# First unit's score products and maxima spread over the last two projection slots, with bands and steps loaded in another order

## The reference

```python
q, k, v = (shape(norm(x) @ W.T) for W in (Wq, Wk, Wv))        # (8, 16, 512, 16)
scores = einsum('bhqd,bhkd->bhqk', q, k) * 16**-0.5 + position_bias(rel_emb)
attn = softmax(scores, axis=-1)
x = x + einsum('bhqk,bhkd->bhqd', attn, v).transpose(...) @ Wo.T
x = x + ffn(norm(x))                                          # two of seven experts and a shared one
```

## Time and profile before

| | |
|---|---|
| median of three runs | 825.53 us (823.11 to 828.63) |
| profiled execution | 820.95 us, of which its span is 819.1 |
| mean granted TensorE clock | 0.958 |
| busy over the span | PE 94%, DVE 76%, PEld 67%, ACT 58%, POOL 32% |
| end of the projection block | 102.46 us from the start of the span |
| first exponent product | 123.69 us |

### The profile page before, as it was taken

How to read it: one execution, slowest core, us unless ns; L and a number is a source line. 1 busy time by engine, 2 the same in 40 slices (tenths; PEclk the granted TensorE clock), 3 DMA queues, 4 the chain that set the end, 5 groups by cost and what they waited for, 6 DMA issues and landing times. The chain is left out here.

```text
span 819.1 us, 18303 instructions
## 1 busy us (share of the span) xinstructions
PE 773.4 (94%) x6261; PEld 551.9 (67%) x6261; DVE 619.1 (76%) x1928; ACT 474.8 (58%) x716; POOL 260.6 (32%) x407
## 2 busy tenths in 40 slices
PE   4899989999999999999999999998997999999997
PEld 2677737566566566566565665777765589999974
DVE  4666487889889889888888884477865567777966
ACT  2344404766766766666666667466454267777730
POOL 1222111121121111111111111237777526666650
PEclk9999956999999999999999999988897999999999
DMA  4899883553364343453345284466632545556769
GB/s 117 229 351 360 304 259 109 135 145 100 101 170 137 116 123 106 151 169 101 99 121 152 81 267 136 166 187 206 212 101 85 175 133 165 161 158 208 222 202 355
DMA packets 74763, 140.77 MB, mean 172 GB/s; under 512 B 14651, under 2 KB 34771, under 8 KB 74497
## 3 DMA queue, kind: packets, MB, share of 16 engines
q1 hardware_dynamic: 62996, 116.12, 46.1%
q0 software_dynamic: 9792, 19.54, 7.4%
q10 hardware_dynamic: 1884, 3.97, 1.4%
HBM read 85.71 MB, written 56.78 MB: 174 GB/s over the span
## 5 line engine op out<-in xcount | busy, mean ns | idle before, releaser
L810 DVE CUSTOM_DVE_ANT_0 sums<-pS,near 128x512 bf16<-128x512 f32 x512 | 329.4, 688 | 48.4 <-PE pS L887 40.0
L847 ACT ACTIVATE prob<-pE 128x1024 f32<-128x1024 f32 x256 | 248.6, 1022 | 152.9 <-PE pE L912 152.8
L912 PEld LDWEIGHTS pE<-bandT,place 64*128 64x128 f32 x2048 | 167.4, 190 | 12.6
L912 PE MATMUL pE<-bandT,place 64*128 64x244 f32 (+2 forms) x2048 | 164.4, 272 | 0.0
L887 PE MATMUL pS<-k_st,q_st 48*128 48x512 f32 x512 | 139.0, 478 | 6.1 <-DVE nmax L810 2.5
L887 PEld LDWEIGHTS pS<-k_st,q_st 48*128 48x128 f32 x512 | 62.8, 193 | 115.6 <-DVE nmax L810 87.8
L926 PE MATMUL pC<-prob,v_aug 128*32 128x512 f32 x1024 | 135.7, 604 | 0.0
L904 PE MATMUL pE<-q_st,k_st 62*128 62x512 f32 x512 | 115.7, 407 | 1.4 <-issue 1.4
L1199 POOL DMA_INDIRECT expert_rows<-rb,xr x76 | 83.7, 1101 | 57.1 <-DVE rb L1414 45.5
L1184 POOL DMA_INDIRECT routed_rows<-xr,slot_i x64 | 66.2, 1034 | 32.2 <-issue 31.3
L1733 PE MATMUL pD<-w2p,hT 128*128 x456 | 63.5, 289 | 0.4 <-DVE hT L1407 0.4
(11 more groups left out here) (202 smaller groups left out, 1066.7 us busy)
## 6 DMA issues: line engine op xcount, KB each, us to landing
xr<-routed_rows SPq DMA_DIRECT2D x38, 258.0 KB, 2.9
q_st<-q_parts SPq DMA_DIRECT2D x64, 128.0 KB, 2.7
k_st<-k_parts SPq DMA_DIRECT2D x64, 128.0 KB, 2.9
ctx<-ctx_sb SPq DMA_DIRECT2D x32, 256.0 KB, 2.7
q_parts<-qk SPq DMA_DIRECT2D x14, 512.0 KB, 7.8
k_parts<-qk SPq DMA_DIRECT2D x14, 512.0 KB, 7.4
near<-bias_by_distance SPq DMA_DIRECT2D x16, 448.0 KB, 5.0
xr<-expert_rows SPq DMA_DIRECT2D x14, 512.0 KB, 4.3
```

The source lines that it names most:

```text
L810: dve.tensor_tensor_reduce(sums[:, r % 4], pS[:, unit % PS], near[:, hg % 2, j, lead:lead + S], -1.0, BIG, ALU.add, ALU.min, nmax[:, j, t: ...
L847: act.activation(prob[:, par, 2 * step:2 * step + 2], pE[:, 2 * (step % 2):2 * (step % 2) + 2], ACT.Exp).then_inc(exp_done, 1)
L912: ins = pe.matmul(pE[:, bank + side, a:z], place[rows, half], bandT[rows, (quad // 2) % 2, pair, part, lead:lead + z - a], start=False, st ...
```

## The change

Unit 0's scores and maxima move to the slots of batches 6 and 7: after each of their 8 groups m, TensorE issues one step of two products into the two banks `pB`, and VectorE takes its two maxima behind the low part of m. A product waits for the maximum two products earlier. `attend` begins with `turn(0)` on VectorE and with unit 1's scores on TensorE. `sums`, `nmax` and the two semaphores are now allocated ahead of both blocks.

SyncE's order is changed with it. The four tables `near` are loaded behind slots 1 to 4 (before, 2 to 5); step 0 behind slot 4, ahead of slot 5's load of x; steps 1 and 2 and the four bands behind slot 6, all within the projection block. In `attend` SyncE waits until unit 0's maxima have landed in the query tile, then loads step 3.

```diff
                 for b in range(B - 1):
                     slot(b, b % 2, b // 2, b < B - 2)
                     if b < 2:
                         load_rows(b)
-                    elif b < 2 + HPG:
-                        if b == 2:
-                            wait_apart(sp, passed, bias_stored, 16 * (4 + FARS))
-                        loads["near"](sp, 0, b - 2)
-                for m in range(4):
-                    wait_apart(sp, passed, qk_out[m], 16 * (B - 2))
-                wait_apart(sp, passed, v_out, 16 * (B - 2))
-                loads["step"](sp, 0, 0, True)
+                    if b == 1:
+                        wait_apart(sp, passed, bias_stored, 16 * (4 + FARS))
+                    if 1 <= b < 1 + HPG:
+                        loads["near"](sp, 0, b - 1)
+                    if b == HPG:
+                        stored(2)
+                        loads["step"](sp, 0, 0, True)
+                loads["step"](sp, 0, 1, True)
+                for j in range(HPG):
+                    loads["band"](sp, 0, j)
+                stored(B - 2)
+                loads["step"](sp, 0, 2, True)
...
                         dve.scalar_tensor_tensor(out=qk[:, m, 1], in0=pQ[:, m % 2, ORDER[m // 2]], scalar=SCALE if m < 2 else 1.0,
                                                  in1=qk[:, m, 0], op0=ALU.mult, op1=ALU.subtract).then_inc(qk_lo, 1)
+                        if first_step is not None:
+                            maxima(first_step + m)
...
+                def maxima(step):
+                    pair, t = divmod(step, TT)
+                    for side in range(2):
+                        unit, j = 2 * step + side, 2 * pair + side
+                        if t == 0:
+                            dve.wait_ge(g["near_ld"][j], 16)
+                        dve.wait_ge(g["s_mm"], unit + 1)
+                        if unit >= 4:
+                            dve.wait_ge(g["max_done"], unit - 3)
+                        lead = P * t
+                        dve.tensor_tensor_reduce(g["sums"][:, unit % 4], pB[:, unit % 2], g["near"][:, 0, j, lead:lead + S], -1.0, BIG,
+                                                 ALU.add, ALU.min, g["nmax"][:, j, t:t + 1]).then_inc(g["max_done"], 1)
...
+                def scores(step):
+                    pair, t = divmod(step, TT)
+                    if step == 0:
+                        pe.wait_ge(g["qk_ld"][0], 16 * 8)
+                        pe.wait_ge(bias_done, 2)
+                    for side in range(2):
+                        unit = 2 * step + side
+                        rows = slice(HALF * side, HALF * side + KQ)
+                        if unit >= 2:
+                            pe.wait_ge(g["max_done"], unit - 1)
+                        pe.matmul(pB[:, unit % 2], g["q_st"][rows, 0, pair, P * t:P * t + P], k_st[rows, 0, pair],
+                                  start=True, stop=True).then_inc(g["s_mm"], 1)
...
@@ attend, sync @@
-                loads["step"](sp, 0, 1, True)
-                for j in range(HPG):
-                    loads["band"](sp, 0, j)
-                for r in range(2, RING):
-                    loads["step"](sp, 0, r, True)
+                sp.wait_ge(max_ld, 32)
+                loads["step"](sp, 0, 3, True)
                 await_stores(sp)
@@ attend, vector @@
-                for ahead in range(STEPS * NI):
+                turn(0)
+                for ahead in range(STEPS, STEPS * NI):
@@ attend, tensor @@
-                for step in range(STEPS + LEAD):
-                    scores(step // STEPS, step // STEPS, 1, step % STEPS)
+                for step in range(LEAD):
+                    scores(1, 1, 1, step)
```

More of the change, by code:

```diff
@@ L189, in layer_kernel @@
             rows_set = sem("rows_set")
+            sums = sb("sums", [P, 4, S], BF16)
+            nmax = sb("nmax", [P, HPG, TT], F32)
+            s_mm, max_done = sem("s_mm"), sem("max_done")
             qk_out = [sem(f"qk_out{m}") for m in range(4)]
@@ L340, in load_rows, with stored @@
                                  ).then_inc(g["rows_set"], 16)
+                def stored(count):
+                    for m in range(4):
+                        wait_apart(sp, passed, qk_out[m], 16 * count)
+                    wait_apart(sp, passed, v_out, 16 * count)
                 for b in range(B - 1):
@@ L419, in normalised_lo, with slot @@
                         dve.tensor_tensor(xT[:, par, 1, c], pT[:, c], xT[:, par, 0, c], ALU.subtract).then_inc(loT, 1)
-                def slot(b, par, i, one, two):
+                def slot(b, par, i, one, two, first_step=None):
                     for m in range(4):
@@ L443, in _ @@
                         slot(2 * i + par, par, i, True, True)
-                slot(B - 2, 0, 3, True, False)
-                slot(B - 1, 1, 3, False, False)
+                slot(B - 2, 0, 3, True, False, 0)
+                slot(B - 1, 1, 3, False, False, TT)
             @block.scalar
@@ L499, in turn, with slot @@
                         ins.then_inc(xT_mm, 1)
-                def slot(b, par, one, first=False):
+                def scores(step):
[10 more added lines that the diff above has]
+                                  start=True, stop=True).then_inc(g["s_mm"], 1)
+                def slot(b, par, one, first=False, first_step=None):
                     pe.wait_ge(loT, 2 * b + 2)
@@ L510, in slot @@
                         ins.then_inc(qk_mm, 1)
+                        if first_step is not None:
+                            scores(first_step + m)
                     if one:
@@ L540, in _ @@
                         slot(2 * i + par, par, True)
-                slot(B - 2, 0, True)
-                slot(B - 1, 1, False)
+                slot(B - 2, 0, True, first_step=0)
+                slot(B - 1, 1, False, first_step=TT)
 def store_qk(engine, g, b, m):
@@ L655, in attend @@
         v_aug = sb("v_aug", [P, 2, TT, HPG, 32], F32)
-        sums = sb("sums", [P, 4, S], BF16)
-        nmax = sb("nmax", [P, HPG, TT], F32)
+        sums, nmax, s_mm, max_done = g["sums"], g["nmax"], g["s_mm"], g["max_done"]
         nparts = sb("nparts", [P, KM, HPG, TT], F32R)
@@ L663, in attend @@
         pC = ps("pC", [P, S], F32)
-        s_mm, max_done, split_done, max_turned, max_out, max_ld = (sem(n) for n in (
-            "s_mm", "max_done", "split_done", "max_turned", "max_out", "max_loaded"))
+        split_done, max_turned, max_out, max_ld = (sem(n) for n in (
+            "split_done", "max_turned", "max_out", "max_loaded"))
         e_mm, exp_done, pv_done, ones_set, v_ready, evac = (sem(n) for n in (
```

## The result

The changed kernel took 833.75 us (median of 13 runs, 824.86 to 841.46) against 822.12 us (818.91 to 830.03) for the kernel before in the same comparison: a ratio of 1.0115, 95% interval 1.0083 to 1.0146. Measured again beside the experiments (after_again), it was 830.66 against 825.04 us, 1.0055 (1.0027 to 1.0084). The ratios are taken over each kernel's fast executions alone, so they are not quotients of these medians. The change makes the kernel slower by some 0.5 to 1.2%. The forecast was 0.24% slower; its range, 820 to 835 us, is -0.7 to +1.15% of 825.53, so the second ratio lies well inside and the first at its very end.

The account below looks back on a forecast made before the run. VectorE's maxima, one pacing each product, were taken to bound the 21.2 us seam between projection and attention. +12.8 for a later block start, -11.5 in the seam, +0.5 near table: +1.8, taken as +2, 827.5 us; range 820 to 835.

Parts of the forecast that it names:

- The deciding step: SyncE's queue: step 0 ahead of x and the query store starts batch 6's first subtraction 2.6 us later, near 87.6.
- the 3.3 us for step 0's 1.0 MB in the transfer engines: Queues before batch 6: 2.6 us at a 512 KB store's pace, taken as 3.3 for smaller pieces, delaying x.
- the 0.5 us for the near table: Queues: one 448 KB table load moves one batch earlier; 0.5 us, between 0 and 1.2.
- The rounds on VectorE: Batch 6's slot: two maxima behind each low-part subtraction, three rounds of 1.95 us plus normalisation; 3.7 us more.
- Rival 2: Batches 6 and 7: the clock falls inside the projection and stays down; some +12 us, 837.5 us; chance 0.10.
- a clock below 1.00 before 105 us: New profile, TensorE's granted clock: listed among the signs that the forecast is wrong.
- SyncE ends the block: Projection's end: 26 issues behind batch 6's value store take 14.9 us; attention starts at 115.3, 12.8 us later.
- The gain in the seam: Projection to first exponents: sixteen maxima and a late landing go; 9.7 us instead of 21.2, -11.5 us.
- The tie: Seam: VectorE's path at 9.5 us against GpSimd's round trip of unit 0's maxima at 9.4 us.
- Rival 1: Queues harmless: step 0 drains in gaps and the block ends by computing; exponents at 118.2, 820 us; chance 0.15.
- rival 3: SyncE's 26 issues run at the loaded pace of 9.7 us a step; +10, 836 us; chance 0.05.

Follow-up runs that it names:

- step0_early: The kernel before with only step 0's loads moved: issued behind slot 4, ahead of slot 5's load of x, instead of behind slot 6; ratio 1.0079.
- near_back: The changed kernel with the four near tables loaded behind slots 2 to 5 again; ratio 1.0049.
- order_only: The changed kernel with unit 0's score products and maxima back in the attention block, SyncE's new order kept; ratio 1.0180.
- fill6: The changed kernel with 24 matmuls without use in TensorE's idle stretches of batch 6's slot; ratio 1.0052.
- half: The changed kernel with only four steps moved, all into batch 7's slot; step 0 behind slot 5, step 1 behind slot 6, other loads as before; ratio 1.0044.
- half_inter: As half, but step 0's loads issued three behind each query or key store of batch 6; ratio 1.0034.
- tail_back: The changed kernel with the bands and step 2 loaded at the start of the attention block again; ratio 1.0053.

## Why the prediction held, and where it was off

**The deciding step was right.** The prediction named step 0's place ahead of the load of x and of the query store as "the step that decides", and step0_early shows that it alone costs 6.6 us. Both waits appeared where they were put, x not before 84 but at 89.4.

**Its size was too small.** The first subtraction was put at 87.6 and came at 91.3 and 90.6. Of the 6.3 us of delay, 2.0 were there at the slot's start and 4.2 in the wait (90.6: 3.5), where the forecast had 0.5 and 2.6. The terms that were too small are the 3.3 us for step 0's 1.0 MB in the transfer engines, and the 0.5 us for the near table. The 3.3 came from the pace of a 512 KB store, 1.3 us. From 81 to 87 us the engines moved 192 GB/s at a share of 1.02; at that rate 1.0 MB takes some 5.3 us, an estimate. That is 2.0 more than the 3.3, where the wait was longer than forecast by 1.6 us (0.9 in after_again). The moved near table cost 1.4 us at the slot's start (near_back).

**The rounds on VectorE** came out near the forecast: from the first subtraction to batch 7's slot 12.0 us (after_again 11.7), forecast 11.4. But order_only, with no maxima in that stretch, took 10.1 and before 7.6, so beside the fall of the clock the maxima added only some 2 us; the forecast had put all 3.7 us on them. In fill6, with maxima and filling and without the fall, it took 11.6. The two costs overlap, and that the sum came out near the forecast is in part luck.

**Rival 2 came true in its short form.** The clock fell in batch 6's slot, for 3.4 to 6.8 us, in every kernel that loads step 0 ahead of that slot or around its start, but for fill6. In half it fell in batch 7's slot, where the wait had moved, and in half_inter in neither. The forecast had named a clock below 1.00 before 105 us as a sign of being wrong, and this sign came (93.9 us); it had allowed up to 5 us for one short fall in its range. In fill6 its removal brought nothing that can be told.

**SyncE ends the block**, as forecast: 4.8 us after ScalarE's copy (over 4 forecast). Its string took 16.7 us instead of 14.9. Since that hangs on batch 6's value store at 104.1 instead of 99.8, the block ended at 121.5 instead of 115.3.

**The gain in the seam** was sized well: 21.2 to 10.3 us, forecast 9.7 with 9.5 to 10.7 as ends. The tie was decided by the round trip (waits of 0.2 and 0.4 us), and in tail_back, where more transfers meet it, it becomes a wait of 4.3 us.

**The sum** by the profile: +19.0 us on the block's start (+12.8 and 0.5 forecast), -10.9 in the seam (-11.5), in all +8.1 instead of +1.8. Of the 6.3 us by which this missed, 3.1 are the two terms of step 0 and the near table, 1.8 SyncE's string, 0.6 the rounds and 0.6 the seam (0.2 are left over by rounding and the block's end): all in one direction, and the time stayed within the range because the range was wide, not because the sum was close. By the runs the whole is +0.55 and +1.15%, 4.5 and 9.5 us, against the 2 forecast. Rival 1, harmless queues, is refuted by step0_early; rival 3, a string at 9.7 us a step, did not come. What stays open is why the same kernel gave 1.0115 in one comparison and 1.0055 in the other, and how much the later return of the clock (half clock through 152 us in the first profile, but only to about 135 in the second and 136 before) adds to it.

## What to carry to other kernels

Before an early load is called free, read how full the issuing queue and the transfer engines are at the new place: in this pipeline, whose queue is nearly full, eleven small issues ahead of one critical load cost 6.6 us by themselves, and the whole new order cost 15.4, where the work that it let start early gave back 7.3 to 7.9. Count what stands on a queue behind the last result before a barrier as part of the block, even if nobody needs it there. And when one wait is removed, look for the one that was nearly as late: here four stood within a few us of each other, SyncE's string, the maxima's round trip, VectorE's rounds and x.

## What the runs showed of the hardware that was not expected

Transfer engines that are fully busy can move half of what they moved just before: 192 GB/s at a share of 1.02 for 6 us while the near table (448 KB) and the step's loads of 48 to 128 KB pass, 407 at 1.05 with the 512 KB stores. In the kernel before, with a near table and no step in flight, it was 186 at 0.96. In half_inter, with the same loads issued between stores, it was 355 at 1.02 (87 to 97 us). What in these loads lowers the rate was not tried.

TensorE's busy share in the seam says little of its clock. With the added matmuls it was busy for 87% of 21.2 us and the granted clock still fell to 1.2 GHz, at 105.6 us, as it did with 82% at 105.0. In batch 6's slot 24 matmuls of another shape (128 rows, against 48 in the seam) in the idle stretches kept it at 2.4 GHz; there TensorE was busy throughout the slot (17.64 of 17.64 us). Which of these differences matters was not tried.
